# Half of the expert blocks take their score rows by DMA, in groups of six

## The reference, cut to what matters

```
logits = jnp.einsum('bsd,ed->bse', x, gate_w)
top_logits, indices = jax.lax.top_k(logits, 6)
scores = jax.nn.softmax(top_logits, axis=-1)
W_sel = lattice_weights[indices]
xW = jnp.einsum('bsd,bskde->bske', x, W_sel)
lattice_out = jnp.einsum('bske,bsk->bse', xW, scores)
proj = jnp.einsum('bsd,ed->bse', lattice_out, out_w) + out_b
```

## Time and profile before

| | |
|---|---|
| median of three runs | 1521.6 us (1521.37 to 1524.91) |
| profiled execution, its own time | 1521.73 us |
| its span | 1520.0 us |
| mean granted TensorE clock | 0.992 |
| PE busy | 1371.7 us, 90% |
| DVE busy | 1183.7 us, 78% |
| POOL busy | 92.4 us, 6% |
| first spread of the expert stage | 1344.5 us |
| end of the last gather | 1506.3 us |

### The profile page before, as it was taken

The page is one execution under the profiler, slowest core; times in us unless marked ns, Lnnn a source line. Parts: engine busy times, 40 slices in busy tenths (PEclk is TensorE's granted clock), DMA queues, the critical chain, the costliest instruction groups (busy, mean ns, idle before and its releaser), DMA issues. The chain is left out here.

```text
span 1520.0 us, 68982 instructions
## 1 busy us (share of the span) xinstructions
PE 1371.7 (90%) x32216; PEld 699.5 (46%) x32216; DVE 1183.7 (78%) x1451; ACT 532.2 (35%) x673; POOL 92.4 (6%) x45
## 2 busy tenths in 40 slices
PE   9889989998899999989999998888789999889996
PEld 3444444445444444454444445555531128843332
DVE  3489999997999999879999997665511118967886
ACT  2522222222222222132222223343379994511211
POOL 1000000000000000000000000000000000045551
PEclk9999999999999999999999999999999999989998
DMA  6233343336766666566666664688844521065420
GB/s 232 90 142 141 131 152 120 135 131 212 277 243 254 246 251 249 195 241 250 257 244 256 243 257 148 252 326 318 342 175 159 181 70 60 8 151 134 118 77 15
DMA packets 55614, 284.35 MB, mean 187 GB/s; under 512 B 16224, under 2 KB 18208, under 8 KB 25504
## 3 DMA queue, kind: packets, MB, share of 16 engines
q1 hardware_dynamic: 34352, 162.22, 32.0%
q10 hardware_dynamic: 21104, 119.76, 19.3%
HBM read 160.33 MB, written 121.63 MB: 186 GB/s over the span
## 5 line engine op out<-in xcount | busy, mean ns | idle before, releaser
L951 ACT ACTIVATE act_c<-slots,conv_b 128x1024 f32<-128x1024 f32 x234 | 258.7, 1115 | 657.4 <-PE slots L603 657.2
L826 DVE STREAM_TRANSPOSE inv_out<-slots 128x1024 f32<-128x1024 f32 x256 | 304.8, 1229 | 77.3 <-PE slots L565 77.3
L603 PEld LDWEIGHTS slots<-inv_w,inv_out 64*64 64x64 f32 x16384 | 268.7, 135 | 194.8 <-issue 184.4
L603 PE MATMUL slots<-inv_w,inv_out 64*64 64x64 f32 x16384 | 299.3, 223 | 14.5 <-issue 8.8
L802 DVE STREAM_TRANSPOSE turned_h<-slots 128x1024 f32<-128x1024 f32 x200 | 237.6, 1227 | 23.7 <-PE slots L498 23.6
L498 PE MATMUL slots<-turned_w,fwd_w 32*64 32x512 f32 x3200 | 204.8, 608 | 22.5 <-DVE inv_out L826 17.2
L777 DVE STREAM_TRANSPOSE turned_w<-act_c 128x1024 f32<-128x1024 f32 x186 | 219.7, 1223 | 0.0
L565 PE MATMUL slots<-turned_k,inv_h 64*64 64x320 f32 x2048 | 167.1, 439 | 36.4 <-DVE turned_h L802 24.4
L587 PE MATMUL slots<-xin,conv_w 32*32 32x512 f32 x3072 | 112.8, 604 | 29.3 <-DMA xin<-act_scratch 15.0
L510 PE MATMUL slots<-turned_h,fwd_h 64*64 64x320 f32 x1600 | 132.8, 443 | 2.1 <-DVE turned_h L802 1.3
L565 PEld LDWEIGHTS slots<-turned_k,inv_h 64*64 64x64 f32 x2048 | 68.1, 132 | 116.3 <-DVE turned_h L802 71.5
(11 more groups left out here) (179 smaller groups left out, 1173.8 us busy)
## 6 DMA issues: line engine op xcount, KB each, us to landing
act_scratch<-act_c ACTq DMA_DIRECT2D x113, 1024.0 KB, 4.1
xin<-act_scratch SPq DMA_DIRECT2D x96, 1024.0 KB, 4.9
act_c<-act_scratch SPq DMA_DIRECT2D x17, 1024.0 KB, 4.9
mode_w<-in_sw_dram SPq DMA_DIRECT2D x20, 640.0 KB, 4.6
at_turned<-level_scratch SPq DMA_DIRECT2D x24, 256.0 KB, 4.1
at_ret_t<-level_scratch SPq DMA_DIRECT2D x20, 256.0 KB, 4.2
xin<-in_x_dram SPq DMA_DIRECT2D x4, 1024.0 KB, 8.6
turned_w<-in_x_turned_dram SPq DMA_DIRECT2D x3, 1024.0 KB, 4.9
```

What stands on the lines that cost most here:

```text
L603: mm = nc.tensor.matmul(banks[half * 64:(half + 1) * 64, 2 * two + odd, at:at + 64], inv_out[rows, t % 2, i, two, s, 2 * half:2 * half + 2 ...
L826: nc.vector.transpose(dst, src).then_inc(inv_turned, 1)
L951: nc.scalar.activation(home[:, :, at, :].rearrange("p i q m -> p q i m"), banks[:, at, :].rearrange("p q (i m) -> p q i m", i=2), ACT.Gelu ...
```

## The change

Every odd block now gets its rows by DMA (`by_dma`): 64 blocks in place of 32. Of these GpSimd still weighs N % 4 == 1, and VectorE weighs the others (N % 4 == 3), from SBUF, in one instruction of 1024 elements (`weigh_rows`). The 64 even blocks are spread by PE and weighed by VectorE in halves, as before. Groups have six blocks, so a group again has three spread blocks; VectorE takes the even blocks of a group first and then its odd ones (`DVE_BLOCKS` is sorted so). SP loads rows for all odd blocks through the same ring of six. The projection, the layer norm steps and their places by N are the same.

```diff
-GROUP_OF = 4
+GROUP_OF = 6
+def by_dma(N):
+    return N % 2 == 1
 def on_pool(N):
-    return N % GROUP_OF == 1
+    return N % 4 == 1
-DVE_BLOCKS = [N for N in range(BLOCKS) if not on_pool(N)]
+DVE_BLOCKS = sorted([N for N in range(BLOCKS) if not on_pool(N)], key=lambda N: (N // GROUP_OF, by_dma(N), N))
+DMA_BLOCKS = [N for N in range(BLOCKS) if by_dma(N)]
+PE_BLOCKS = [N for N in range(BLOCKS) if not by_dma(N)]
...
-            for i, N in enumerate(POOL_BLOCKS):
+            for i, N in enumerate(DMA_BLOCKS):
                 g = N // EB
                 if i >= ROWS_RING:
-                    sp.wait_ge(weigh_pool, i - ROWS_RING + 1)
+                    before = DMA_BLOCKS[i - ROWS_RING]
+                    if on_pool(before):
+                        sp.wait_ge(weigh_pool, after_weigh_pool(before))
+                    else:
+                        sp.wait_ge(weigh, after_weigh(before, 0))
...
+            def weigh_rows(N):
+                i, g = DMA_BLOCKS.index(N), N // EB
+                dve.wait_ge(rows_in[i % ROWS_RING], 32 * (i // ROWS_RING + 1))
+                if N >= WB:
+                    dve.wait_ge(gathered, N - WB + 1)
+                nc.vector.tensor_tensor(weighted[N % WB], rows_of[i % ROWS_RING], y_t[:, g * SLOT:(g + 1) * SLOT],
                                         ALU.mult).then_inc(weigh, 1)
...
-            for N in range(BLOCKS):
+            for N in DVE_BLOCKS:
                 g, n = N // EB, N % EB
-                if not on_pool(N):
+                if by_dma(N):
+                    weigh_rows(N)
+                else:
                     for half in range(2):
                         weigh_half(N, half)
```

More of the change, by code:

```diff
@@ L1057, in expert_pairs @@
         pairs = iter([EB // 4 * r + n for n in range(EB // 4) for r in range(4)])
-        for pool in (False, True):
+        for dma in (False, True):
             for N in range(g * EB, (g + 1) * EB):
-                if on_pool(N) == pool:
+                if by_dma(N) == dma:
                     pair_of[N] = next(pairs)
@@ L1168, in after_weigh @@
         def after_weigh(N, half):
-            return 2 * DVE_BLOCKS.index(N) + half + 1
+            return sum(1 if by_dma(n) else 2 for n in DVE_BLOCKS[:DVE_BLOCKS.index(N)]) + half + 1
         def after_weigh_pool(N):
@@ L1307, in spread_half @@
             def spread_half(N, half):
-                i, g = DVE_BLOCKS.index(N), N // EB
+                i, g = PE_BLOCKS.index(N), N // EB
                 if i >= PB:
-                    pe.wait_ge(weigh, 2 * (i - PB) + half + 1)
+                    pe.wait_ge(weigh, after_weigh(PE_BLOCKS[i - PB], half))
                 at, r = g * SLOT + half * 512, PAIR_OF[N] // (EB // 4)
@@ L1324, in gather @@
                 else:
-                    pe.wait_ge(weigh, after_weigh(N, 1))
+                    pe.wait_ge(weigh, after_weigh(N, 0 if by_dma(N) else 1))
                 if N == 0:
@@ L1409, in spread_group @@
                     for N in range(q * GROUP_OF, min((q + 1) * GROUP_OF, BLOCKS)):
-                        if not on_pool(N):
+                        if not by_dma(N):
                             spread_half(N, half)
@@ L1547, in weigh_half @@
                                         slots[:, i % PB, half * 512:(half + 1) * 512], y_t[:, at:at + 512],
+                                        ALU.mult).then_inc(weigh, 1)
+            def weigh_rows(N):
[4 more added lines that the diff above has]
+                nc.vector.tensor_tensor(weighted[N % WB], rows_of[i % ROWS_RING], y_t[:, g * SLOT:(g + 1) * SLOT],
                                         ALU.mult).then_inc(weigh, 1)
@@ L1839, in _ @@
                 g = N // EB
-                pool.wait_ge(rows_in[i % ROWS_RING], 32 * (i // ROWS_RING + 1))
+                k = DMA_BLOCKS.index(N)
+                pool.wait_ge(rows_in[k % ROWS_RING], 32 * (k // ROWS_RING + 1))
                 if N >= WB:
@@ L1845, in _ @@
                     pool.wait_ge(moved[e], n)
-                nc.gpsimd.tensor_tensor(weighted[N % WB], rows_of[i % ROWS_RING], y_t[:, g * SLOT:(g + 1) * SLOT],
+                nc.gpsimd.tensor_tensor(weighted[N % WB], rows_of[k % ROWS_RING], y_t[:, g * SLOT:(g + 1) * SLOT],
                                         ALU.mult).then_inc(weigh_pool, 1)
```

## The result

The changed kernel takes 1535.25 us (median of five executions, 1530.59 to 1538.32), against 1521.6 us before (five, 1518.97 to 1524.91). The ratio is 1.0084, with a 95% interval of 1.0059 to 1.0110: slower by some 13 us. I had predicted 1524.3 us, with 1515 to 1532 as the range, and "no difference" as the likeliest. The forecast was wrong: the change costs five times what I gave it.

The account below looks back on a forecast made before the run. PE was taken to bound the kernel, 1.063 us a block. First projection at 1397.4, two chunks of 39.5 and a last stretch of 32.5 put the last gather at 1508.9, 2.6 us later: 1524.3 us, range 1515 to 1532.

Parts of the forecast that it names:

- PE's terms: Expert stage, PE: 12.08 us per 12 blocks, 2.2 for the projection, 1.85 lost behind it; 37.4 us a chunk undisturbed.
- The start: Up to the first projection, transfers saturated at 237 GB/s set the pace; it begins at 1397.4, 1.8 us later.
- DVE beside POOL: DVE's new weighs with two SBUF inputs meeting POOL's weighs: 0.45 us each taken, between nothing and 0.69.
- W: Price per new 1024-wide DVE weigh of meeting POOL: 0.45 us taken, giving DVE 12.15 us per 12 blocks.
- the term of 3.15 us a chunk: Further layer norm steps on DVE, per chunk: 0.2, 0.2, 1.15, 0.75 and 0.85 us.
- The bound: Upper case for W: DVE waits for the whole POOL instruction it meets, 0.69 us on average; 1530.3 us in all.
- The slack: DVE's spare time beside PE: 1.3 us per 12 blocks at W = 0, gone at W = 0.45.
- the clock: PE's clock: no cost for a fall behind the start; a fall while waiting for rows would refute the prediction.
- Rival C: POOL bars DVE for its whole weigh, at each group's odd weighs; 0.69 us each, 1526.3 to 1533 us, chance 0.24.
- A: The forecast itself: DVE and POOL partly hold each other up, saved spreads and slower start cancel; 1521 to 1527.5 us, chance 0.42.
- the mean of the new weigh: Mean of DVE's new 1024-wide weigh in the profile after: 1.6 us in A, 1.9 in Rival C.
- three signs of being wrong: Row transfers above 237 GB/s, first projection before 1395.5, or PE's clock falling in gaps where it waits for rows.

Follow-up runs that it names:

- e1: Changed kernel, but from block 12 on GpSimd multiplies only 16 of the 1024 columns of its blocks; 1514.3 us, ratio 0.9978 to the kernel before.
- e9: Changed kernel with GpSimd multiplying 16 columns from block 12 and VectorE's odd blocks reading one constant buffer, so 32 row pairs load; ratio 0.9965 to before.
- e3: Kernel before, with the half weighs of blocks N % 4 == 3 reading a constant SBUF buffer in place of their PSUM slot; ratio 1.0298.
- e4: Kernel before, with GpSimd taking two of every five blocks in place of one of four, in groups of five; 1547.4 us, ratio 1.0216.
- e2: Changed kernel, but VectorE's odd blocks read one constant SBUF buffer, so only GpSimd's 32 blocks load by DMA; 1528.7 us, ratio 1.0063 to before.
- e5: Changed kernel, with the two 8-element TENSOR_SCALARs of the layer norm steps on ScalarE in place of VectorE; ratio 1.0071 to the kernel before.
- e8: Changed kernel, with each GpSimd weigh of 1024 columns split into two of 512; ratio 1.0088 to the kernel before.

## Why the prediction was wrong

- **PE's terms were right.** 12.08 us per 12 blocks, 2.2 for the projection and 1.85 behind it gave 37.4 us a chunk for an undisturbed VectorE; e1 has 37.7 and 36.5, and its stage is 3.0 us shorter than before where the sum had 3.4. That it is so close is in part luck: e1 has half clock around 1398 to 1400 us and again around 1474, which the sum had not.
- **The start was right.** The first projection 1.8 us later, by saturated transfers at 237 GB/s: measured 1.8 us, 239 GB/s. The price of transfers up to there was larger than the some 2 us that I read from the sum for e9: 4.9 us between e1 and e9, where GpSimd is out of the way.
- **The step that failed is "DVE beside POOL".** Three things in it. *What it was applied to:* I gave the price W to the 32 new weighs alone and took the layer norm steps at their old durations, in the term of 3.15 us a chunk. In the changed kernel the five kinds that L1612, L1597, L1602, L988 and L1616 stand for take 11.9 us more over three chunks, 4.0 a chunk, more than the weighs' 10. Before, no small step fell into a GpSimd weigh, and I read their 0.16 us as what they cost, not as what they cost in that phase. W itself, 0.45, was too high: 0.32 measured. *The bound:* I took the average of a random meeting, 0.69 us, as the most. With a fixed phase it isn't: e3 has 1.4 us a block. The proper bound was the whole of the longest run of GpSimd instructions, and e4 has 10.7 us. *The slack:* a held-up instruction also moves what VectorE does next. Both chunks and the last stretch together came out 11.6 us over the forecast's sum.
- **A term at nothing: the clock.** The sum took PE at full clock throughout. Behind its waits for VectorE PE had half clock in four stretches; 2.6 us of that stand in the chain, at most some 6.8 us in all.
- **Rival C** had the mechanism and the place, with 0.24, and 1530.3 us; it shares the first two faults and the clock, and so stops short too. That I gave it less than A was a judgement that no row supported.
- **What would show it:** I had named the mean of the new weigh as the sign, 1.6 us for A and 1.9 for C. It was 1.53, nearer to A than to C, and the time was beyond C's centre. The sign looked at one line only. Of the three signs of being wrong, the clock came true, though PE waited for VectorE and not for rows. The rate was 239 GB/s and not 237, which changes nothing. The first projection, at 1391.94, is before 1395.5 by the time of day, but only because the stage began 5.4 us earlier: counted from there it is later.

What stays open: how the 14.3 us of the stage divide between weighs, steps, clock and transfers. e2 and e5 show that they aren't additive, since removing one moves the others to another phase, and transfers belong to it, for in the changed kernel they set when most of GpSimd's weighs start. Why a TENSOR_SCALAR on eight columns doesn't get in between back-to-back GpSimd weighs in e4 wasn't tried. It isn't always so: in the changed kernel one L1612 (1398.61, 1.18 us) ended at 1399.79 between two additions of GpSimd that follow on each other at 1399.72.

## What to carry to other kernels

Before VectorE is given an instruction with a second SBUF input, or left with a small one, beside a busy GpSimd, ask what GpSimd runs at that moment: an eight-column step cost 0.16 us before and up to 10.7 us beside other GpSimd work (e4). A hold-up of this kind stands in the trace as busy time, never as a wait, so compare the longest duration of a group with its shortest before trusting its mean. When one engine's input source is changed, price every instruction that shares the new resource, the old ones too, and by the longest run of the other engine, not by its average. And where TensorE has been made to wait, look at the granted clock behind the wait: six gathers took 7.0 us there and 5.3 elsewhere.

## What the runs showed of the hardware that I had not expected

- An eight-column TENSOR_SCALAR on VectorE waited 10.7 us, through five GpSimd weighs without a gap (e4), while a 1024-column TENSOR_TENSOR got its turn after one 512-column instruction (e8: 2.37 us for 1.12).
- GpSimd is held up as well: its weigh took 3.41 us and not 2.37 behind a VectorE weigh, its 512-column additions 1.77 us on average and not 1.28.
- An eight-column RECIPROCAL inside a GpSimd weigh took 0.18 to 0.19 us in all three chunks of the changed kernel, as it does elsewhere.
- Behind waits for VectorE, TensorE's granted clock was 0.50 in four stretches of the changed kernel's stage and in none of the kernel before behind 1360 us.
- Reading one input from SBUF and not from PSUM, in 64 of 192 half weighs, made the kernel 3.0% slower, and 1.7% when it was the neighbouring blocks.
